# Expert stage of an attention and mixture-of-experts block: rings of gathered rows and output tiles from 12 to 6 tiles, weight ring from 4 to 3

## The reference

```python
h = _layernorm(x) * (1 + cb) + sb
logits = xt @ Wg                      # (4096, 8)
probs = softmax(logits)
_, top_idx = top_k(probs.T, cap)      # every expert picks 512 tokens
...
tok2exp = where(assigned, argmax(masked), argmax(pT))   # one expert for each token
for e in range(E):
    gate = where(tok2exp == e, weights, 0.0)
    y = gelu(xt @ W1[e]) @ W2[e]      # 128 -> 256 -> 128
    out = out + gate[:, None] * y
x = x + gb * out
```

## Time and profile before

| | us |
|---|---|
| median of three runs | 358.38 |
| lowest and highest run | 358.21, 360.11 |
| span of the profiled execution, first to last instruction | 353.6 |
| outside that span, taken from the median | 4.8 |
| first gather of the expert stage | 224.03 |
| first scatter | 242.83 |
| last gather | 325.74 |
| last scatter | 345.90 |

### The profile page before, as it was taken

The page is one execution under the profiler, slowest core; times in us unless marked ns, Lnnn a source line. Parts: engine busy times, 40 slices in busy tenths (PEclk is TensorE's granted clock), DMA queues, the critical chain, the costliest instruction groups (busy, mean ns, idle before and its releaser), DMA issues.

```text
span 353.6 us, 4547 instructions
## 1 busy us (share of the span) xinstructions
PE 200.0 (57%) x1081; PEld 165.5 (47%) x1082; DVE 213.8 (60%) x691; ACT 112.2 (32%) x374; POOL 187.3 (53%) x224
## 2 busy tenths in 40 slices
PE   0949578979848674322444202358463848357770
PEld 0527457767645573312434101258362737346750
DVE  3779953389999997478767789714231414324360
ACT  1366442544534411003535000214132324224440
POOL 7315963155566673995000009575757566675552
PEclk9999899998987955555555555565858676588695
DMA  5940000010000000365000000131212121222100
GB/s 157 308 129 3 0 1 2 0 31 2 0 0 3 1 0 2 99 194 152 1 0 0 0 1 0 48 101 62 66 59 68 46 80 49 59 67 46 45 27 0
DMA packets 17700, 16.88 MB, mean 48 GB/s; under 512 B 2333, under 2 KB 14752, under 8 KB 17680
## 3 DMA queue, kind: packets, MB, share of 16 engines
q1 hardware_dynamic: 13568, 9.18, 8.5%
q0 software_dynamic: 3120, 7.22, 7.0%
q10 hardware_dynamic: 992, 0.27, 0.6%
HBM read 10.36 MB, written 6.75 MB: 48 GB/s over the span
## 4 chain that ended last, share of the span: by engine, by line
issue 27%; POOL 21%; PE 21%; DVE 16%; another core or an unknown queue 4%; ACT 4%; DMA 2%; ACTq 2%; POOLq 1%; SPq 0%; DVEq 0%
DVE x_sb L895 9%; PE pH L695 9%; POOL yr L242 3%; PE pQ L704 3%; POOL h L288 3%; POOL t L287 3%; DVE bn L743 3%; POOL featT L307 3%; POOL rs L242 2%; POOL out_dram L318 2%; PE pH L597 2%; ACTq L451 2%; POOL t L253 1%; POOL x_sb L255 1%
## 5 line engine op out<-in xcount | busy, mean ns | idle before, releaser
L695 PE MATMUL pH<-u,hid 128*128 128x128 f32 x156 | 36.9, 379 | 36.1 <-issue 22.3
L1098 DVE SCALAR_TENSOR_TENSOR qp<-pQ,wslot,qp 128x128 f32<-128x128 f32 x39 | 13.7, 350 | 71.1 <-remote 37.8
L318 POOL DMA_INDIRECT out_dram<-u,sidx x39 | 39.5, 1013 | 31.6 <-DVE u L1103 20.0
L695 PEld LDWEIGHTS pH<-u,hid 128*128 128x128 f32 x156 | 30.2, 272 | 40.9 <-issue 40.8
L314 POOL DMA_INDIRECT xn<-table_dram,gidx x39 | 40.2, 1030 | 14.9 <-issue 11.0
L704 PE MATMUL pQ<-ew,u 128*128 x156 | 35.1, 364 | 6.3 <-issue 5.6
L895 DVE SCALAR_TENSOR_TENSOR x_sb<-u,yr,x_sb 128x128 f32<-128x128 f32 x64 | 34.0, 591 | 4.6 <-POOL yr L242 4.3
L456 ACT ACTIVATE u<-pH 128x256 f32<-128x256 f32 x39 | 14.9, 383 | 61.7 <-remote 40.6
L704 PEld LDWEIGHTS pQ<-ew,u 128*128 128x128 f32 x156 | 28.9, 261 | 11.2 <-issue 10.7
L307 POOL TENSOR_SCALAR featT<-iota,lo 128x128 bf16<-128x128 bf16 x8 | 9.4, 1184 | 46.6 <-DVE hi L1049 46.6
L452 ACT COPY hid<-ew 128x256 f32 x39 | 15.8, 405 | 42.7 <-issue 42.7
(11 more groups left out here) (258 smaller groups left out, 508.2 us busy)
## 6 DMA issues: line engine op xcount, KB each, us to landing
x_sb<-in_L_attn_x_dram SPq DMA_DIRECT2D x8, 256.0 KB, 8.1
table_dram<-x_sb SPq DMA_DIRECT2D x8, 256.0 KB, 2.8
table_dram<-h SPq DMA_DIRECT2D x8, 256.0 KB, 2.3
ew<-in_L_ffn_W_dram SPq DMA_DIRECT2D x1, 1024.0 KB, 9.2
ew<-in_L_ffn_W_dram SPq DMA_DIRECT2D x2, 512.0 KB, 9.9
xn<-table_dram,gidx POOLq DMA_INDIRECT x39
out_dram<-u,sidx POOLq DMA_INDIRECT x39
wmod_sb<-in_L_wmod_dram SPq DMA_DIRECT2D x1, 384.0 KB, 4.6
```

What stands on the lines that cost most here:

```text
L318: gp.indirect_dma_start(out.rearrange("b l d -> (b l) d"), bass.IndirectOffsetOnAxis(sidx[:, j:j + 1], 0), o_sb[:, j % R, :], None, bounds ...
L695: mm = te.matmul(pH[k % 2][:, f * P:(f + 1) * P], wcur[:, k % RW, f * P:(f + 1) * P], xt[:, k % 2, :], start=True, stop=True)
```

## The change

Two numbers change. `R` sets the number of slots of `row` and of `o_sb`, how many gathers POOL issues before the first scatter, which scatter DVE waits for, and how many tiles a loop body of PE, ACT and DVE holds. `RW` sets the number of slots of `wcur`. `NL`, the number of tiles that the loops cover, stays at 36: six rounds of six tiles in place of three rounds of twelve.

```diff
@@ -30,8 +30,8 @@
 DV = 5
 EARLY = 4
 NJ = NT + E - 1
-R = 12
-RW = 4
+R = 6
+RW = 3
 POOLQ = 3
 NL = NJ // R * R
```

## The result

The changed kernel takes 362.06 us (median of 20 runs, 358.76 to 364.88). The kernel before, run in turn with it, takes 359.61 us (20 runs, 356.91 to 362.01). The ratio is **1.0057, with a 95% interval of 1.0034 to 1.0080**: a little slower. It goes by the runs within 1.5% of the fastest of their kernel, which leaves out three of the changed one; the medians of all runs give 1.0068. A second group of runs gave 1.0044 (0.9999 to 1.0088).

What follows compares the result with a forecast made beforehand. It took PE's results, held back while POOL issues indirect DMAs without pause, to set 3.14 us per tile. −6.1 + 6.4 + 1.7 + 1.5 = +3.5 us gave span 357.1, with 4.8 outside 361.9 us; range 355 to 369.

Steps and rivals of the forecast that it cites:

- the likeliest case: The prediction's own sum of all terms: slower than before, at 359 to 365 us; chance 0.38.
- Start of the stage: Before the first scatter: POOL stops after six gathers, PE's results come sooner, first scatter at 236.7; −6.1 us, other bound 0.
- six fewer gathers save no time of their own: Ahead of the first scatter: no separate gain, since POOL was idle for 3.05 us there before.
- Six more tiles at the gathering pace: Scatters 26 to 32 now carry a gather each, 3.14 us for a tile where 2.07 before: +6.4 us, at least +3.5.
- The drain: The only six scatters left after the last gather may be of the slower kind: 0 to +3.4, taken as +1.7 us.
- A gather just in time: At round starts, gathers land about 0.6 us late for PE's transposes: 0 to +3.3 us, taken as +1.5.
- Loops and weight ring: Three more loop turns on PE, ACT and DVE and the smaller weight ring cost 0, at most +0.7 us.
- 4.8 us outside the span: Gap between the traced span, 353.6 us, and the median run, 358.38 us, added unchanged at the end.
- results are released when POOL stops: In the expert stage, PE's held results reach DVE 1.5 us after POOL falls idle, seen in two places.
- rival A: The expert stage's start doesn't get faster, as PE's results are late for a reason of their own: 368.0 us; chance 0.13.
- Rival B: The short ring holds PE to POOL's pace and late results become rarer: faster, 343.7 us if all went; chance 0.20.
- Rival D: Gathers late by over a landing time, each round's 3 us wait spread over four tiles, not five: 367 us; chance 0.09.

## Why the prediction was right

The number, the sign and the likeliest case held: 361.9 us forecast and 362.06 measured. The median of the kernel before rose to 359.61 with more runs, so the difference that I forecast as +3.5 us is +2.45 by the medians and +3.9 and +1.7 in the two pairs of traces. That the total agrees to 0.2 us is luck: a base that was 1.2 us too low and a difference that was 1 us too high cancel. Term by term:

- **Start of the stage, −6.1.** Measured −6.6 (18.8 to 12.2) in both pairs. The size was right and the reason only in part. The first scatter stands behind twelve gathers in POOL's queue, which take 14.76 us up to the start of the last and 1.3 for that one. It can't come before about 16.1, and in the short setting, with no held results, it comes at 16.2. So results in time would have given 2.6 us without the change, and the other 4.0 need the six gathers out of the way as well. My sentence that six fewer gathers save no time of their own holds only as long as the result is late; the term of 6.1 us needed both.
- **Six more tiles at the gathering pace, +6.4.** Measured +6.8 and +5.7.
- **The drain, +1.7.** Measured +3.4 and +1.9, up to the upper bound. The last gather stands 11 us ahead of the last scatter, not 9.
- **A gather just in time, +1.5.** Too large. The waits are there, 3.5 us in four cases with 1.6 as the longest, but the pace up to scatter 26 moved from 3.14 and 3.12 to 3.15 and 3.15, which is 0.2 to 0.8 us over 26 tiles.
- **Loops and weight ring, 0.** Shown in the short setting, where POOL is the bound; not run in the long one.
- **4.8 us outside the span.** Wrong. The traced execution of the changed kernel has both a time and a span, 362.23 and 360.4, which is 1.8 us. By that the traced execution of the kernel before took about 355.4 us (an estimate), less than any of the 20 runs. The forecast went right because it was the median plus a difference.

That PE's results are held while POOL issues indirect DMAs was argued from one place at the start. In the long setting the late results at the start went in both traces of the changed kernel, and the kernel in which POOL is silent has none in the silent stretch, where the clock changed too; the 95 us at 0.50 show that a low clock isn't enough. My reading that results are released when POOL stops is right for some only. In the changed kernel too DVE gets one 1.6 us after POOL ends a row of pairs (253.80 behind 252.23). But the gelu of the earlier trace rows at 272.99 starts while POOL issues a scatter, and in the earlier trace rows DVE's copy at 235.56 comes 4.2 us before the twelve gathers end. The rule of the Trainium skill, page "SBUF — State Buffer", section "Who interferes with whom", that DMA never contends with a compute engine, isn't what decides the time here: rival A, which followed from it, needed a first scatter 18.8 us after the first gather, and it came after 12.2. But the runs don't show that SBUF's ports are the place. They show that the late results come only in stretches with POOL's indirect DMAs, in one setting and not in the other. What the DMAs have to do with it, their preparation on POOL or the data that they move, wasn't tested. Rival B, a faster kernel because the ring paces PE, fell: DVE's late waits are 39.9 and 39.8 us against 37.8 and 29.0. Rival D fell with the pace.

What I hadn't seen is what the change costs at its root. I reasoned about an early start and a late end at a given pace. The short setting shows it without the held results: a ring that is half as deep leaves POOL idle at both ends of the stage, and the time of POOL's queue is the least that this stage can have. In the long setting POOL waits for late results anyhow: beyond the 0.3 us between two DMAs it is idle for 20.0 and 21.8 us with twelve slots and for 23.5 and 23.0 with six, where the short setting has 0.4 and 6.7. That part of the idle time is free there, and hence 2 us in place of 5, is my reading of these sums.

## What to carry to other kernels

The depth of a ring counts at the two ends of a stage before it counts in the middle: reckon what the queue that issues the transfers may do before the first result, and how much it still has to do behind the last transfer. A first output that comes early is no gain where the issuing queue is the bound, because that queue has merely been idle. And when a wait has no releaser that fits, look at what each other engine does when it begins and ends, and leave that engine's work out once; a stall that goes with another engine's work can be absent altogether when the same kernel runs on another chip or at another time.

## What the hardware did that I had not expected

The same kernel took 359.6 and 357.8 us in two groups of runs and 337.9 and 338.4 us in two others. In the long setting PE's results came up to 6 us late while POOL issued gathers and scatters, and a tile took 3.14 us. In the short setting none came late in the same code and a tile took 2.67 us. The clock by itself isn't the cause: the gathering stretch had 0.70 in the one and 0.79 in the other, but 95 us at 0.50 ahead of the expert stage had no late result. With POOL silent there was none either, nor in a row of twelve scatters at 1.00. The mechanism, and what puts a run into one setting or the other, stays open.
